# Attention outputs and softmax sums regrouped by DMA in place of two TensorE transposes

## The reference

```
xn = layernorm(x)
q, k, v = split(xn @ Wqkv);  Q, K = rope(q), rope(k)
y = softmax(mask(Q K^T / sqrt(8))) V          # 16 heads of 8
attn = y @ Wproj
mlp = (silu(xn @ Wg + bg) * (xn @ Wu + bu)) @ Wd + bd
experts: top 8 of key sums, softmax weights, silu(xn . down_e) * up_e
out = x + attn + mlp + experts
```

## Time and profile before

| | |
|---|---|
| median of three runs | 770.66 us |
| the profiled execution | 770.97 us |
| its span in the profile | 769.2 us |
| PE busy | 688.9 us (90%) |
| DVE busy | 613.1 us (80%) |
| ACT busy | 539.0 us (70%) |
| POOL busy | 414.4 us (54%) |
| TensorE clock granted, mean | 0.953 of full speed |

### The profile page before, as it was taken

How to read it: one execution, slowest core, us unless ns; L and a number is a source line. 1 busy time by engine, 2 the same in 40 slices (tenths; PEclk the granted TensorE clock), 3 DMA queues, 4 the chain that set the end, 5 groups by cost and what they waited for, 6 DMA issues and landing times.

```text
span 769.2 us, 15222 instructions
## 1 busy us (share of the span) xinstructions
PE 688.9 (90%) x5756; PEld 280.9 (37%) x5756; DVE 613.1 (80%) x1292; ACT 539.0 (70%) x824; POOL 414.4 (54%) x547
## 2 busy tenths in 40 slices
PE   3976688898889899999798999999999999999997
PEld 2442133333333434443233343443233433333343
DVE  4569989999878998998688996789966799784532
ACT  3342166259999768637698776574988668999982
POOL 5463277477887795378357615158400136764840
PEclk9988579899999999999999999999999999999999
DMA  6536003133000010025400002520300001000000
GB/s 140 103 63 86 3 1 42 31 55 71 1 2 1 1 31 28 3 38 68 90 2 1 5 1 32 74 48 16 56 2 2 1 1 31 3 1 4 2 1 28
DMA packets 33814, 22.48 MB, mean 29 GB/s; under 512 B 6380, under 2 KB 33388, under 8 KB 33740
## 3 DMA queue, kind: packets, MB, share of 16 engines
q1 hardware_dynamic: 32876, 20.72, 15.7%
q10 hardware_dynamic: 864, 0.79, 0.6%
HBM read 6.23 MB, written 2.10 MB: 11 GB/s over the span
## 4 chain that ended last, share of the span: by engine, by line
PE 42%; DVE 23%; ACT 10%; issue 8%; POOL 8%; DMA 4%; SPq 3%; ACTq 1%; POOLq 0%; DVEq 0%
DVE pmax L1115 14%; PE ybank L1350 10%; PE banks L1382 7%; ACT pT L965 6%; PE banks L1327 6%; DVE wsum L1183 4%; PE banks L1403 4%; PE banks L1298 4%; SPq L677 3%; PE banks L1275 2%; POOL ssum L829 2%; ACT wsum L1008 2%; POOL coef L846 2%; DMA qs<-negmaxT 2%; PE banks L1336 2%
## 5 line engine op out<-in xcount | busy, mean ns | idle before, releaser
L1115 DVE TENSOR_REDUCE pmax<-banks 128x2 f32<-128x1024 f32 (+3 forms) x304 | 344.3, 1161 | 42.1 <-PE banks L1308 24.0
L965 ACT ACTIVATE pT<-banks 128x1024 f32<-128x1024 f32 (+3 forms) x384 | 295.8, 830 | 57.8 <-PE banks L1336 39.0
L829 POOL TENSOR_TENSOR ssum<-sim 128x512 f32<-128x512 f32 x128 | 144.8, 1136 | 123.0 <-DVE wsum L1183 63.1
L1350 PE MATMUL ybank<-pT,vaug 128*32 128x512 f32 (+3 forms) x1536 | 167.0, 510 | 0.7 <-ACT pT L965 0.2
L1298 PE MATMUL banks<-ks,qs 48*128 48x512 bf16 (+3 forms) x768 | 117.4, 346 | 32.8 <-DVE pmax L1115 25.8
L1327 PE MATMUL banks<-qs,ks 51*128 51x512 bf16 (+3 forms) x768 | 122.9, 337 | 21.7 <-ACT pT L965 9.1
L1183 DVE SCALAR_TENSOR_TENSOR wsum<-ssum,best,wsum 128x512 f32<-128x512 f32 x128 | 122.5, 971 | 11.0 <-ACT wsum L1008 10.8
L1008 ACT ACTIVATE wsum<-ssum,wbias 128x512 f32<-128x512 f32 x128 | 92.9, 742 | 26.4 <-POOL ssum L829 21.2
L846 POOL TENSOR_TENSOR coef<-coef,wsum 128x512 f32<-128x512 f32 x64 | 87.0, 1360 | 33.8 <-DVE wsum L1183 32.7
L1327 PEld LDWEIGHTS banks<-qs,ks 51*128 51x128 bf16 x768 | 36.7, 94 | 154.9 <-ACT pT L965 107.3
L1298 PEld LDWEIGHTS banks<-ks,qs 48*128 48x128 bf16 x768 | 32.9, 96 | 129.0 <-DVE pmax L1115 71.1
(11 more groups left out here) (113 smaller groups left out, 834.4 us busy)
## 6 DMA issues: line engine op xcount, KB each, us to landing
ks<-parts SPq DMA_DIRECT2D x90, 64.0 KB
qs<-parts SPq DMA_DIRECT2D x90, 64.0 KB
xin<-in_L_attn_x SPq DMA_DIRECT2D x4, 512.0 KB, 4.8
osb<-in_L_attn_x SPq DMA_DIRECT2D x8, 256.0 KB, 2.8
out<-osb SPq DMA_DIRECT2D x8, 256.0 KB, 2.3
ks<-parts ACTq DMA_DIRECT2D x6, 64.0 KB
qs<-parts ACTq DMA_DIRECT2D x6, 64.0 KB
qs<-negmaxT SPq DMA_DIRECT2D x16, 24.0 KB
```

The costliest lines, as they stand in the source:

```text
L829: g.tensor_tensor(ssum[:, m % NSS, :, :], s[:, h, 0:XI].unsqueeze(2).to_broadcast([P, XI, NKEYS]), s[:, RH + h:RH + h + 1, :].to_broadcast ...
L965: a_.activation(pT[:, q % NPT, 2 * e:2 * e + 2, q0:CHUNK], pair(("sc", *n))[:, :, q0:CHUNK], ACT.Exp, scale=SCALE).then_inc(out_sem, 1)
L1115: v.tensor_reduce(pmax[:, c, i % TPC, k0 // CHUNK, :].rearrange("p (e j) -> p e j", e=2) [:, :, js[0]:js[-1] + 1], pair(("mx", b, c, k))[: ...
L1350: ins = t_.matmul(ybank[32 * j:32 * j + 32, q0:CHUNK], vaug[:, b % 2, kt, v0:v0 + 32], pT[:, q % NPT, j, q0:CHUNK], start=kt == 0, stop=kt ...
```

## The change

The transposes yt and yo, the copy Yo and the normalization ym go. A new SP task `yg.b.c.two` follows two groups' Yc: four transfers lay the heads' rows of y side by side in yz[:, 0], and two transfers write each head's sum of weights eight times into yz[:, 1], so that each row of y has its sum on its own partition. When both yg of a stage have landed, DVE's new task `yd.b.c` takes the reciprocal of yz[:, 1] (128x512) and multiplies it into yz[:, 0], and ac.4 reads the result there. The rows come in another order than before, so the rows of Wproj are loaded in that order, by two transfers in place of one. A buffer of yT4 is free again when the rows of yg have landed, no longer after yt; yz is one buffer, so yg waits for ac.4 of the stage before.

```diff
+                elif kind == "yg":
+                    c, two = n
+                    for gr in (2 * two, 2 * two + 1):
+                        w.wait_ge(done["Yc"], rank("Yc", b, c, gr))
+                    if serial(b, c) > 0:
+                        w.wait_ge(done["ac"], rank("ac", *STAGES[serial(b, c) - 1], NF))
+                    r = HALF * two
+                    for j in range(4):
+                        sp.dma_start(yz[r + 2 * DH * j:r + 2 * DH * (j + 1), 0, :], yT4[32 * j:32 * j + DH, :, :])\
+                            .then_inc(y_rows_loaded, 16)
+                    for e in range(2):
+                        sp.dma_start(yz[r + e:r + HALF:2, 1, :],
+                                     yT4[DH::32, e, :].unsqueeze(1).to_broadcast([4, DH, CHUNK]))\
+                            .then_inc(y_rows_loaded, 16)
...
                     if k >= 2:
-                        w.wait_ge(done["yt"], rank("yt", *GROUP_ORDER[k - 2]))
+                        w.wait_ge(y_rows_loaded, y_rows(*GROUP_ORDER[k - 2]))
                     a_.activation(yT4[:, k % 2, :], ybank[:, :], ACT.Copy).then_inc(out_sem, 1)
...
+                elif kind == "yd":
+                    b, c = n
+                    for gr in range(GROUPS):
+                        w.wait_ge(y_rows_loaded, y_rows(b, c, gr))
+                    s = mark(v.reciprocal(yz[:, 1, :], yz[:, 1, :]))
                     need(s)
-                    v.tensor_tensor(ytm[:, :, 4 * gr:4 * gr + 4, :], wv[:, :, :, 0:DH],
-                                    yinv[:, k % 2, :, :].unsqueeze(3).to_broadcast([P, TPC, 4, DH]), ALU.mult)\
-                        .then_inc(out_sem, 1)
+                    v.tensor_tensor(yT, yT, yz[:, 1, :], ALU.mult).then_inc(out_sem, 1)
...
-                        (wproj_sb[:, :], wproj),
+                        (wproj_sb[0:HALF, :], wproj[0:HALF, :].rearrange("(g j d) n -> j d g n", g=2, j=4)),
+                        (wproj_sb[HALF:P, :], wproj[HALF:P, :].rearrange("(g j d) n -> j d g n", g=2, j=4)),
```

More of the change, by code:

```diff
@@ new lines @@
+pv.0.0.0.2 sc.0.0.0.3.1@23 mx.0.1.15@45 sm.0.4@6 mx.0.1.16@01 mx.0.1.17@23 sc.0.0.1.0.0@45 pv.0.0.0.3 sc.0.0.1.0.1@45
+mx.0.1.18@01 sc.0.0.1.1.0@45 pv.0.0.1.0 sc.0.0.1.1.1@45 sc.0.0.1.2.0@23 mx.0.1.19@01 sc.0.0.1.2.1@45 pv.0.0.1.1
+mx.0.1.20@23 mx.0.1.21@01 sc.0.0.1.3.0@45 pv.0.0.1.2 sm.0.5@6 mx.0.1.22@23 sc.0.0.1.3.1@45 sc.0.0.2.0.0@01
+sc.0.0.2.0.1@45 pv.0.0.1.3 mx.0.1.23@23 mx.0.1.24@01 sc.0.0.2.1.0@45 pv.0.0.2.0 mx.0.1.25@23 sc.0.0.2.1.1@45
+sc.0.0.2.2.0@01 sc.0.0.2.2.1@45 mx.0.1.26@23 mx.0.1.27@01 pv.0.0.2.1 sc.0.0.2.3.0@45 pv.0.0.2.2 sm.0.6@6
@@ new lines @@
+pv.1.0.0.0 sc.1.0.0.2.0@23 mx.1.1.13@45 sm.1.5@6 mx.1.1.14@01 sc.1.0.0.2.1@23 sc.1.0.0.3.0@45 pv.1.0.0.1
+sc.1.0.0.3.1@23 sc.1.0.1.0.0@45 pv.1.0.0.2 sc.1.0.1.0.1@23 pv.1.0.0.3 mx.1.1.15@01 sc.1.0.1.1.0@45 sc.1.0.1.1.1@23
+ac.0.1.0@6 sc.1.0.1.2.0@01 mx.1.1.16@45 mx.1.1.17@23 pv.1.0.1.0 pv.1.0.1.1 mx.1.1.18@01 sc.1.0.1.2.1@45 ac.0.1.1
+sc.1.0.1.3.0@23 sc.1.0.1.3.1@45 pv.1.0.1.2 sc.1.0.2.0.0@23 sc.1.0.2.0.1@45 pv.1.0.1.3 mx.1.1.19@01 ac.0.1.2
+sc.1.0.2.1.0@23 ac.0.1.3 sc.1.0.2.1.1@45 mx.1.1.20@01 mx.1.1.21@23 pv.1.0.2.0 sc.1.0.2.2.0@45 sc.1.0.2.2.1@01
@@ new lines @@
+gt.1.1.2@3 sc.1.1.0.0.0@01 sc.1.1.0.0.1@56 up.1.1.0@2 up.1.1.3@4 up.1.1.1@3 up.1.1.2@2 sc.1.1.0.1.0@01 mx.2.0.0@34
+sc.1.1.0.1.1@56 pv.1.1.0.0 sc.1.1.0.2.0@01 mx.2.0.1@23 sc.1.1.0.2.1@45 pv.1.1.0.1 sc.1.1.0.3.0@01 mx.2.0.2@23
+sc.1.1.0.3.1@45 pv.1.1.0.2 sc.1.1.0.4.0@01 mx.2.0.3@23 sc.1.1.0.4.1@45 pv.1.1.0.3 sc.1.1.0.5.0@01 mx.2.0.4@23
+sc.1.1.0.5.1@45 pv.1.1.0.4 sc.1.1.0.6.0@01 sc.1.1.0.6.1@23 mx.2.0.5@45 pv.1.1.0.5 pv.1.1.0.6 sc.1.1.0.7.0@01
+sc.1.1.0.7.1@23 mx.2.0.6@45 sc.1.1.1.0.0@01 sc.1.1.1.0.1@23 pv.1.1.0.7 sm.2.1@6 sc.1.1.1.1.0@01 mx.2.0.7@45
@@ new lines @@
+sc.1.1.3.5.1@23 mx.2.1.3@45 pv.1.1.3.4 sc.1.1.3.6.0@01 sc.1.1.3.6.1@23 mx.2.1.4@45 ct.1.1.3@6 sc.1.1.3.7.0@01
+pv.1.1.3.5 sc.1.1.3.7.1@01 mx.2.1.5@23 sc.2.0.0.0.0@45 pv.1.1.3.6 pv.1.1.3.7 sc.2.0.0.0.1@01 mx.2.1.6@23 mx.2.1.7@45
+ct.1.1.0@6 xt.3@01 mx.2.1.8@23 mx.2.1.9@45 sc.2.0.0.1.0@01 pv.2.0.0.0 mx.2.1.10@23 sc.2.0.0.1.1@01 sc.2.0.0.2.0@45
+sc.2.0.0.2.1@01 pv.2.0.0.1 sc.2.0.0.3.0@23 mx.2.1.11@01 mx.2.1.12@45 pv.2.0.0.2 sc.2.0.0.3.1@23 ac.1.1.0@6
+sc.2.0.1.0.0@01 sc.2.0.1.0.1@23 qk.3.1.1@45 qk.3.1.0@01 sc.2.0.1.1.0@23 sc.2.0.1.1.1@45 pv.2.0.0.3 ac.1.1.1
@@ new lines @@
+mx.2.1.42@01 mx.2.1.43@23 ac.2.0.2 ac.2.0.3 mx.2.1.44@01 ac.2.0.4 mx.2.1.45@23 ac.2.0.5 mx.2.1.46@01 ac.2.0.6
+mx.2.1.47@23 ac.2.0.7 mx.2.1.48@01 ac.2.0.8 mx.2.1.49@23 dn.2.1.2@6 mx.2.1.50@01 dn.2.1.0@5 mx.2.1.51@23 ot.2.0@6
+mx.2.1.52@01 dn.2.1.3@5 mx.2.1.53@23 dn.2.1.1@6 gt.2.1.3@5 sm.2.4@6 mx.3.1.0@01 mx.3.1.1@23 gt.2.1.1@5 mt.2.1@6
+mx.3.1.2@01 sm.2.6@4 mx.3.1.3@23 gt.2.1.2@6 mx.3.1.4@01 gt.2.1.0@5 mx.3.1.5@23 up.2.1.2@6 sc.2.1.0.0.0@45
+sc.2.1.0.0.1@01 up.2.1.1@6 mx.3.1.6@23 sc.2.1.0.1.0@45 sc.2.1.0.1.1@01 pv.2.1.0.0 sc.2.1.0.2.0@23 mx.3.1.7@45
@@ new lines @@
+sc.2.1.0.2.1@01 pv.2.1.0.1 sc.2.1.0.3.0@23 up.2.1.3@6 sc.2.1.0.3.1@01 sc.2.1.0.4.0@23 mx.3.1.8@45 pv.2.1.0.2
+sc.2.1.0.4.1@01 pv.2.1.0.3 sc.2.1.0.5.0@23 mx.3.1.9@45 sc.2.1.0.5.1@01 pv.2.1.0.4 sc.2.1.0.6.0@23 sc.2.1.0.6.1@01
+pv.2.1.0.5 mx.3.1.10@45 sc.2.1.0.7.0@23 sm.2.7@6 sc.2.1.0.7.1@01 sc.2.1.1.0.0@23 mx.3.1.11@45 pv.2.1.0.6
+sc.2.1.1.0.1@01 pv.2.1.0.7 sc.2.1.1.1.0@23 mx.3.1.12@45 sc.2.1.1.1.1@01 pv.2.1.1.0 sc.2.1.1.2.0@23 mx.3.1.13@45
+sc.2.1.1.2.1@01 pv.2.1.1.1 sc.2.1.1.3.0@23 mx.3.1.14@45 sc.2.1.1.3.1@01 pv.2.1.1.2 sc.2.1.1.4.0@23 mx.3.1.15@45
@@ new lines @@
+pv.3.1.1.1 sc.3.1.1.2.1@01 sc.3.1.1.3.0@23 mx.3.0.9@45 sc.3.1.1.3.1@01 pv.3.1.1.2 sc.3.1.1.4.0@23 mx.3.0.10@45
+sc.3.1.1.4.1@01 pv.3.1.1.3 mx.3.0.11@23 sc.3.1.1.5.0@45 sc.3.1.1.5.1@01 pv.3.1.1.4 sc.3.1.1.6.0@23 mx.3.0.12@45
+sc.3.1.1.6.1@01 pv.3.1.1.5 sc.3.1.1.7.0@23 mx.3.0.13@45 pv.3.1.1.6 sc.3.1.1.7.1@01 sc.3.1.2.0.0@23 sm.3.2@6
+sc.3.1.2.0.1@01 mx.3.0.14@45 sc.3.1.2.1.0@23 pv.3.1.1.7 ct.3.1.1@6 sc.3.1.2.1.1@01 pv.3.1.2.0 sc.3.1.2.2.0@23
+mx.3.0.15@45 sc.3.1.2.2.1@01 pv.3.1.2.1 sc.3.1.2.3.0@23 mx.3.0.16@45 sc.3.1.2.3.1@01 pv.3.1.2.2 sc.3.1.2.4.0@23
@@ new lines @@
+mx.3.0.17@45 sc.3.1.2.4.1@01 pv.3.1.2.3 sc.3.1.2.5.0@23 mx.3.0.18@45 sc.3.1.2.5.1@01 pv.3.1.2.4 sc.3.1.2.6.0@23
+sc.3.1.2.6.1@01 pv.3.1.2.5 sc.3.1.2.7.0@23 mx.3.0.19@45 sc.3.1.2.7.1@01 pv.3.1.2.6 sc.3.1.3.0.0@23 sc.3.1.3.0.1@01
+pv.3.1.2.7 mx.3.0.20@45 ct.3.1.2@6 sc.3.1.3.1.0@23 mx.3.0.21@45 sc.3.1.3.1.1@01 pv.3.1.3.0 sc.3.1.3.2.0@23
+sc.3.1.3.2.1@01 pv.3.1.3.1 ct.3.1.0@6 sc.3.1.3.3.0@23 mt.3.0@5 sc.3.1.3.3.1@01 pv.3.1.3.2 sc.3.1.3.4.0@23
+sc.3.1.3.4.1@01 pv.3.1.3.3 sc.3.1.3.5.0@23 sm.3.3@6 sc.3.1.3.5.1@01 sc.3.1.3.6.0@23 pv.3.1.3.4 sc.3.1.3.6.1@01
@@ new lines @@
+pv.3.1.3.5 sc.3.1.3.7.0@23 sc.3.1.3.7.1@01 pv.3.1.3.6 sc.3.0.0.0.0@23 sc.3.0.0.0.1@01 pv.3.1.3.7 ct.3.1.3@6
+sc.3.0.0.1.0@23 sc.3.0.0.1.1@01 pv.3.0.0.0 sc.3.0.0.2.0@23 sc.3.0.0.2.1@01 pv.3.0.0.1 sc.3.0.0.3.0@23 sc.3.0.0.3.1@01
+pv.3.0.0.2 sc.3.0.1.0.0@23 sc.3.0.1.0.1@01 pv.3.0.0.3 sc.3.0.1.1.0@23 sc.3.0.1.1.1@01 pv.3.0.1.0 sc.3.0.1.2.0@23
+sc.3.0.1.2.1@01 pv.3.0.1.1 sc.3.0.1.3.0@23 ac.3.1.0@6 pv.3.0.1.2 sc.3.0.1.3.1@01 sc.3.0.2.0.0@23 ac.3.1.1
+sc.3.0.2.0.1@01 sc.3.0.2.1.0@23 pv.3.0.1.3 ac.3.1.2 sc.3.0.2.1.1@01 pv.3.0.2.0 sc.3.0.2.2.0@23 sc.3.0.2.2.1@01
@@ new lines @@
+ex.2.1.1.0.1 ex.2.1.1.1.0 ex.2.1.1.1.1 we.2.5.3 ex.2.1.1.2.0 ex.2.1.1.2.1 ex.2.1.1.3.0 ex.2.1.1.3.1 Sm.2.7
+ex.2.1.1.4.0 ex.2.1.1.4.1 we.2.6.0 ex.2.1.1.5.0 we.2.6.1 ex.2.1.1.5.1 we.2.6.2 ex.2.1.1.6.0 ex.2.1.1.6.1 be.2.7
+ex.2.1.1.7.0 ex.2.1.1.7.1 we.2.6.3 ex.2.1.2.0.0 ex.2.1.2.0.1 Yc.2.1.1 ln.2.7 ex.2.1.2.1.0 ex.2.1.2.1.1 we.2.7.0
+ex.2.1.2.2.0 ex.2.1.2.2.1 we.2.7.1 ex.2.1.2.3.0 ex.2.1.2.3.1 ex.2.1.2.4.0 we.2.7.2 we.2.7.3 Sm.3.5 ex.2.1.2.4.1
+ex.2.1.2.5.0 Sm.3.4 ex.2.1.2.5.1 ex.2.1.2.6.0 ex.2.1.2.6.1 ex.2.1.2.7.0 ex.2.1.2.7.1 ex.2.1.3.0.0 ex.2.1.3.0.1
@@ L381 @@
+nr.1.1 so.1.0 xr.2.0 ga.2.1.0 ga.2.1.1 yg.1.1.0 nr.2.0 yg.1.1.1 ga.3.1.0 yg.2.0.0 ga.3.1.1 so.1.1 xr.2.1 yg.2.0.1
+ga.3.0.1 so.2.0 xr.3.0 nr.2.1 yg.2.1.0 yg.2.1.1 ga.3.0.0 so.2.1 nr.3.1 xr.3.1 yg.3.1.0 nr.3.0 yg.3.1.1 yg.3.0.0 so.3.1
+yg.3.0.1 so.3.0
 """
@@ L539, in build @@
         yT4 = sb("yT4", [P, 2, CHUNK])
-        ytm = sb("ytm", [P, TPC, H, DH])
-        yinv = sb("yinv", [P, 2, TPC, 4])
-        yT = sb("yT", [P, CHUNK])
+        yz = sb("yz", [P, 2, CHUNK])
+        yT = yz[:, 0, :]
         hT = sb("hT", [P, NF, CHUNK])
@@ L592, in build @@
         NFIRST = 3
-        NWEIGHTS = 11
+        NWEIGHTS = 12
         NCONST = 3
@@ L613, in rank, with y_rows @@
             return RANK[task]
+        def y_rows(b, c, gr):
+            return 16 * 6 * (GROUP[b, c, gr] // 2 + 1)
         def rows(b, c, a):
@@ L971, in _ @@
                     if k >= 2:
-                        w.wait_ge(done["yt"], rank("yt", *GROUP_ORDER[k - 2]))
+                        w.wait_ge(y_rows_loaded, y_rows(*GROUP_ORDER[k - 2]))
                     a_.activation(yT4[:, k % 2, :], ybank[:, :], ACT.Copy).then_inc(out_sem, 1)
-                elif kind == "Yo":
-                    b, c = n
```

(33 more changed lines are left out.)

546 lines of the change are left out of this document (245 added, 301 removed), and 7 rows, old and new, of the table KINDS.

## The result

The changed kernel takes 785.97 us (median of 4 runs, 783.73 to 788.05) against 769.84 for the kernel before (767.44 to 770.99). The ratio is 1.0213, 95% interval 1.0169 to 1.0258: slower by about 16 us. The profiled execution is the slowest of the four (788.05). Ratios leave out runs over 1.5% slower than the fastest of their kernel, four of the twelve of the last experiment and none elsewhere. The forecast of 765.5 and its range up to 780 were wrong. The rival that named the reciprocal where VectorE is full was the right one, and it was priced too low (778.5).

A forecast was written before the change was run, and what follows sets the result against it. No single engine was taken to set the end, with PE on half of the chain and DVE full at stage ends. Terms -12 + 4 - 0.5 + 1 + 2 = -5.5 us gave 765.5 us, range 750 to 780 (own range 755 to 767).

The forecast's parts named there:

- the term of VectorE: VectorE: 64 small instructions traded for 16 long ones, 12 us net gained, a third reaching the end: +4 us.
- The cover that I named: Behind yd at stage ends: PE has other matrices written between and three pairs to fill ahead while reductions wait.
- ACT at -0.5: ScalarE: loses the copy Yo, 8 times 0.59 us, one of them where ACT is full: -0.5 us.
- PE, -12: TensorE: 40 tasks of four transposes go, 25.9 us of busy time; -12 us, with ends 0 and -25.9.
- The reciprocal, 3.0: VectorE: price of one 128x512 reciprocal, the largest unknown, taken as 3.0 us between 0.76 and 4.0.
- y's path, +1, and the SP queue: Last pv to ac.4: 96 more SP transfers, path 10.8 us, just covered by other work; +1 us (0 to +14).
- rival *no change: PE gets only -9.6 us and transfers come late, one uncovered wait of 7 us: about 772 us; chance 0.26.
- The tail, +2 net: After the last Yc: path 4.5 us longer, half of 4.5 us PE work moved from mid-stage given back: +2 us.
- The slower rival: Reciprocal of 4.0 us at six stage ends where DVE is full, two thirds uncovered, +17: 778.5 us; chance 0.26.
- rival *cheap reciprocal: Reciprocal at 0.76 us, DVE loses 5.9 us net, PE's 19.2 us come through whole: 750 us; chance 0.12.

The follow-up runs named there:

- the last experiment: Changed kernel with the inverse made on ScalarE (exp of minus the logarithm) and yd left at its written place: 771.19 us, 0.9993 of the kernel before.
- the cheap reciprocal: Changed kernel with a multiplication in place of each reciprocal (sums squared, not inverted): 760.94 us, 0.9895 of the kernel before.
- in one block: Kernel before plus seven unread reciprocals of 48 elements per stage, one behind the other after the last ym: 791.52 us, ratio 1.0306.
- spread out: Kernel before plus seven unread reciprocals of 48 elements per stage, one ahead of each of the next seven VectorE tasks: 784.94 us, ratio 1.0197.
- one experiment: Changed kernel with yd two tasks later in VectorE's list in seven stages and behind hu in the last: 791.4 us, 1.0313 of the kernel before.

## Why the prediction was wrong

*The step that failed* is the weight in the term of VectorE: "I let a third of the net reach the end: +4 us". The net of the instructions traded was nearly right (12 us predicted, 26.8 + 6.5 - 17.4 = 15.9 from the rows). But a long instruction was set off against short ones elsewhere. The new instructions stand where DVE is full and are paid whole and more: with the cheap reciprocal six stages gave back 21 us for some 14 us of VectorE's time (2.4 us each). The cover that I named, matrices written between and three pairs to fill ahead, was for the most part not there: in one block 93% came through, and spread out still 63%. What the 17.4 us of small instructions gave back no run isolates. With PE at -10.5, ACT at -0.5, y's path at 0 and the tail at +6, some +21 is left for VectorE in a change of +16. Seven yd at 4.2 us are 29, six without that of (3,1) 25, so between 4 and 8 of the 17 came back, by an estimate in which PE's term alone is uncertain by 5.

*PE, -12:* right by size, -10.5. Its busy time was to be near 663 us and that of DVE near 625; they are 685.6 and 640.5, and 669.1 and 625.5 with the cheap reciprocal. DVE's busy time grew by 27.4 and not by 15.9, since instructions that nobody touched got longer too: the 128 of wsum (L1183, now L1188) take 128.2 us where they took 122.5, with the cheap reciprocal 129.6. *The reciprocal, 3.0:* 3.35, the forecast's own band of 2.5 to 3.5. The Trainium skill's repeat count of 8 (VectorE: DVE Perf Modes, the walkthrough of the 8-slice pipeline) at a cycle of its 0.96 GHz each would give an estimated 4.3 us; the trace doesn't agree with that at 3.35 us, and agrees that the operation is dear by the element: (3350 - 252) / 496 = 6.2 ns, against 1.02 for a multiplication.

*y's path, +1, and the SP queue:* covered as predicted. From the end of yd to the stage's first product with wproj it is 6.8 to 21.9 us in the seven stages, and DMA and the SP queue have 1% each of the chain. The late nr of the rival *no change* showed in one experiment, not in the changed kernel. (Four yg stand right behind a ga in the SP list, not five as I counted.)

*The tail, +2 net:* the path grew by 8.3 us instead of 4.5. The 0.7 us of the rows' landing and 0.5 of yd are small; two hu written behind yd left PE idle for 4.16 us, and the eight products behind that took 2.9 us longer. Against the 2.25 us that gt and up were to give back, the term is +6.

*The slower rival* had the place right, six stage ends, and "two thirds uncovered" too low, with nothing for the tail beyond +2. The windows had shown it: with DVE at 18.4 to 20 of 20, PE's larger total over the whole run was no argument for cover there. I used it as one. The rival *cheap reciprocal* was priced too well: with 0.95 us in place of 3.35 the kernel took 761 us, not 750.

## What to carry to other kernels

Weigh added and removed time stage by stage, not as a net: what was added to an engine that is full in a window counted whole here or more, and what leaves it elsewhere must not be set off against that unseen. Before an elementwise inverse is made wide, look at its price by the element; here the same inverse was cheaper on the engine that had room. A chain of waits lists candidates; the stage times with and without a step are its price.
